# First cross attention: two heads in two row halves of TensorE, scores in two accumulated steps

## The reference

```python
def _L0_xattn_ref(q, k, v, Wq, bq, Wk, bk, Wv, bv, Wo, bo):   # q = layernorm(x), k = v = ctx_512 (4 x 4096 x 128)
    HEADS, D_K = 16, 16
    ...
    scores = jnp.einsum('bhqd,bhkd->bhqk', qh, kh) * scale
    attn = jax.nn.softmax(scores, axis=-1)
    out = jnp.einsum('bhqk,bhkd->bhqd', attn, vh)
```

## Time and profile before

| what | us |
|---|---|
| median of 3 runs | 1431.14 (1427.41 to 1432.78) |
| span of the profiled execution | 1429.1 |
| busy PE | 1375.6 |
| busy DVE | 1055.1 |
| busy ACT | 922.1 |
| busy POOL | 287.6 |

### The profile page before, as it was taken

How to read it: one execution, slowest core, us unless ns; L and a number is a source line. 1 busy time by engine, 2 the same in 40 slices (tenths; PEclk the granted TensorE clock), 3 DMA queues, 4 the chain that set the end, 5 groups by cost and what they waited for, 6 DMA issues and landing times.

```text
span 1429.1 us, 28070 instructions
## 1 busy us (share of the span) xinstructions
PE 1375.6 (96%) x11138; PEld 846.7 (59%) x11138; DVE 1055.1 (74%) x2114; ACT 922.1 (65%) x1899; POOL 287.6 (20%) x321
## 2 busy tenths in 40 slices
PE   7799999999999999999999999999999999989998
PEld 5355555555555545555554556556557999856666
DVE  4787777787777778777778888835876778767757
ACT  5366777767777767777767666672796664448731
POOL 3354222222222222122213100000003100001210
PEclk9899999999999999999999999999999999999999
DMA  6966555346554545655454743002402320347000
GB/s 184 163 145 143 119 118 111 77 102 130 116 127 92 102 84 125 128 115 113 81 97 101 184 73 61 2 1 60 119 18 65 112 67 1 91 112 155 2 1 30
DMA packets 95587, 133.19 MB, mean 93 GB/s; under 512 B 8864, under 2 KB 70944, under 8 KB 89504
## 3 DMA queue, kind: packets, MB, share of 16 engines
q1 hardware_dynamic: 95456, 131.40, 42.3%
HBM read 94.15 MB, written 37.22 MB: 92 GB/s over the span
## 4 chain that ended last, share of the span: by engine, by line
PE 79%; ACT 8%; DVE 8%; DMA 2%; issue 2%; SPq 1%; POOL 0%; DVEq 0%; ACTq 0%
PE psum L559 16%; PE psum L540 13%; PE psum L524 13%; ACT probs L783 4%; PE psum L2132 4%; PE psum L587 3%; PE psum L2106 3%; DVE peaks L685 3%; PE psum L626 3%; PE psum L1226 2%; PE psum L2851 2%; PE psum L1623 1%; PE psum L275 1%; PE psum L2861 1%; PE psum L2814 1%
## 5 line engine op out<-in xcount | busy, mean ns | idle before, releaser
L685 DVE TENSOR_REDUCE peaks<-psum 128x1 f32<-128x512 f32 x1024 | 643.3, 684 | 197.0 <-PE psum L524 196.4
L783 ACT ACTIVATE probs<-psum 128x512 f32<-128x512 f32 x1024 | 529.0, 615 | 83.3 <-PE psum L540 79.4
L524 PE MATMUL psum<-keysT,queriesT 96*128 96x512 bf16 x1024 | 390.1, 384 | 13.2 <-DMA keysT<-key_parts 7.9
L540 PE MATMUL psum<-queriesT,keysT 98*128 98x256 bf16 x2048 | 392.4, 274 | 6.1 <-ACT queriesT L846 2.4
L540 PEld LDWEIGHTS psum<-queriesT,keysT 98*128 98x128 bf16 x2048 | 176.3, 99 | 191.7 <-ACT probs L783 72.1
L559 PE MATMUL psum<-probs,values 128*17 128x256 f32 x4096 | 245.9, 380 | 0.0
L559 PEld LDWEIGHTS psum<-probs,values 128*17 128x17 f32 x4096 | 107.2, 97 | 102.6 <-issue 27.1
L524 PEld LDWEIGHTS psum<-keysT,queriesT 96*128 96x128 bf16 x1024 | 98.6, 96 | 90.9 <-issue 56.1
L918 POOL CAST key_parts<-key_f 128x512 bf16<-128x512 f32 x57 | 34.8, 611 | 518.0 <-ACT key_f L816 511.0
L816 ACT ACTIVATE key_f<-psum,bk 128x512 f32<-128x512 f32 x59 | 40.5, 687 | 120.7 <-PE psum L587 120.6
L587 PE MATMUL psum<-ctxT,wk 128*128 128x512 f32 x128 | 69.5, 625 | 2.4 <-DVE probs L728 0.9
(11 more groups left out here) (315 smaller groups left out, 1662.5 us busy)
## 6 DMA issues: line engine op xcount, KB each, us to landing
keysT<-key_parts SPq DMA_DIRECT2D x31, 768.0 KB, 7.7
key_parts<-key_parts SPq DMA_DIRECT2D x90, 256.0 KB
keysT<-key_parts SPq DMA_DIRECT2D x31, 512.0 KB, 10.1
ctx_nat<-in_ctx_dram SPq DMA_DIRECT2D x32, 256.0 KB, 3.0
keysT<-key_parts SPq DMA_DIRECT2D x31, 256.0 KB, 11.6
ctx_in<-in_ctx_dram SPq DMA_DIRECT2D x24, 256.0 KB, 5.9
ctx_turned<-ctxT SPq DMA_DIRECT2D x24, 256.0 KB, 4.4
ctx_T<-ctx_turned SPq DMA_DIRECT2D x12, 512.0 KB, 3.8
```

Of the source, the lines that this page charges most:

```text
L524: e.matmul(ps, self.queriesT[0:ROWS, u % 2, g * GH + j, t * P:(t + 1) * P], self.keysT[0:ROWS, i % RING, j, c * BANK:(c + 1) * BANK], star ...
L540: made = e.matmul(ps[:, j * S:(j + 1) * S], self.keysT[0:AUG, i % RING, j, kt * P:(kt + 1) * P], self.queriesT[0:AUG, u % 2, g * GH + j, : ...
L685: e.tensor_reduce(self.peaks[:, i % 2, pair, c:c + 1], k.ps(("max", n)), AX.X, ALU.max).then_inc(*self.peaked.up(n))
L783: e.activation(self.probs[:, t % RINGP, e2 * GH * S:(e2 + 1) * GH * S], k.ps(("scores", t, e2)), ACT.Exp).then_inc(*self.exped.up((t, e2)))
```

## The change

Each head gets its own row half of 64 rows. `keysT` and `queriesT` now have two planes: in MAIN four part products of a head (64 rows), in REST the other two part products and the two rows of ones and shift (34 rows). Head 0 lies at row 0, head 1 at row 64. A maximum is found from the MAIN plane alone, so from four part products; the maxima of the two heads follow each other. Scores are made for each head in its own bank (both 128-key tiles of the slot side by side), each in two accumulated steps, MAIN and REST, with the heads alternating; the banks still rotate over three, `SCORES[(2 * t + j) % 3]`. All eight score products of a slot stand ahead of the maxima, and the values burst behind both maxima. An exponential now covers one head of the slot, and each head has semaphores of its own for maxima and for scores. The copy of the turned shift becomes two. The parts are stored in an order in which the high and middle parts of the keys are one run of 32 rows, read twice for MAIN; the parts of the queries are stored five times instead of three.

```diff
-PAIRS = 6
-ROWS = PAIRS * DH
-AUG = ROWS + 2
+KEY_AT = (1, 2, 0)
+QUERY_AT = ((2, 3), (0, 1), (4,))
+HALF = P // 2
+MAIN, REST = 0, 1
+LOW = 2 * DH
+TALL = LOW + 2
...
-HALVES, SUMS = 3, 3
+SCORES, SUMS, BLOCK = (0, 1, 2), 3, 4
...
-        self.keysT = sb(scope, "keysT", [P, RING, GH, LC], BF16)
+        self.keysT = sb(scope, "keysT", [P, 2, RING, LC], BF16)
-        self.queriesT = sb(scope, "queriesT", [P, 2, P // DH, S], BF16)
+        self.queriesT = sb(scope, "queriesT", [P, 2, 2, UNIT_GROUPS, S], BF16)
...
-            i, r = divmod(n, MAXES)
-            pair, c = self.max_at(n)
-            j, t = divmod(pair, QT)
+            i, j, qt, c = self.max_at(n)
             u, g = divmod(i, UNIT_GROUPS)
+            own = slice(j * HALF, (j + 1) * HALF)
             job, let_go = ("max", n), (self.peaked, n)
             ps = banks.use(4 + n % 3, w, job, let_go) if now < -1 else misc(now, job, let_go)
             w.wait_ge(self.rows_here[u % 2], u)
             else:
                 w.wait_ge(self.pieces_here[c * self.PIECES // CH], 0)
-            e.matmul(ps, self.queriesT[0:ROWS, u % 2, g * GH + j, t * P:(t + 1) * P],
-                     self.keysT[0:ROWS, i % RING, j, c * BANK:(c + 1) * BANK],
-                     start=True, stop=True).then_inc(*self.max_made.up(n))
+            e.matmul(ps, self.queriesT[own, MAIN, u % 2, g, qt * P:(qt + 1) * P],
+                     self.keysT[own, MAIN, i % RING, c * BANK:(c + 1) * BANK],
+                     start=True, stop=True).then_inc(*self.max_made[j].up(n))
 
         for t in range(FIRST, TOTAL + 3):
             maxima = self.maxima(t)
...
                 u, g = divmod(i, UNIT_GROUPS)
                 w.wait_ge(self.shiftT_kept, i)
                 w.wait_ge(self.ones_in, 0)
-            for e2 in range(2):
-                if 0 <= t < TOTAL:
-                    kt, n = 2 * p + e2, (2 * t + e2) % HALVES
-                    ps = banks.use(n, w, ("scores", t, e2), (self.exped, (t, e2)))
-                    for j in range(GH):
-                        made = e.matmul(ps[:, j * S:(j + 1) * S], self.keysT[0:AUG, i % RING, j, kt * P:(kt + 1) * P],
-                                        self.queriesT[0:AUG, u % 2, g * GH + j, :], start=True, stop=True)
-                    made.then_inc(*self.scored.up((t, e2)))
-                if maxima and not e2:
-                    find_max(maxima[0], t)
-            if t % 4 == 1 and 5 <= t <= TOTAL + 1:
-                i, p0 = divmod(t - 5, SLOTS)
+                ps = {}
+                for e2 in range(2):
+                    kt = 2 * p + e2
+                    for plane, rows in ((MAIN, HALF), (REST, TALL)):
+                        for j in range(GH):
+                            if j not in ps:
+                                ps[j] = banks.use(SCORES[(2 * t + j) % len(SCORES)], w, ("scores", t, j), (self.exped, (t, j)))
+                            own = slice(j * HALF, j * HALF + rows)
+                            made = e.matmul(ps[j][:, e2 * S:(e2 + 1) * S], self.keysT[own, plane, i % RING, kt * P:(kt + 1) * P],
+                                            self.queriesT[own, plane, u % 2, g, :], start=(plane == MAIN), stop=(plane == REST))
+                            if e2 and plane == REST:
+                                made.then_inc(*self.scored[j].up((t, j)))
+            for n in maxima:
+                find_max(n, t)
+            if t % BLOCK == 1 and BLOCK + 1 <= t <= TOTAL + 1:
+                i, p0 = divmod(t - BLOCK - 1, SLOTS)
                 b, g = divmod(i, NG)
                 w.wait_ge(self.exped, (t - 2, 1))
-                for p in range(p0, p0 + 4):
+                for p in range(p0, p0 + BLOCK):
                     w.wait_ge(self.v_kept, (b, p))
                 w.wait_ge(self.ones_set, b % 2)
                 if i:
                     w.wait_ge(self.outT_kept, i - 1)
                 w.wait_ge(self.cleared, 0)
-                for p in range(p0, p0 + 4):
+                for p in range(p0, p0 + BLOCK):
                     for e2 in range(2):
                         for j in range(GH):
-                            quad, kt = e2 * GH + j, 2 * p + e2
+                            quad, half, kt = e2 * GH + j, 2 * j + e2, 2 * p + e2
                             made = e.matmul(k.bank(SUMS)[32 * quad:32 * quad + DH + 1, 0:S],
                                             self.values[b % 2][:, kt, g * GH + j, :],
-                                            self.probs[:, (SLOTS * i + p) % RINGP, quad * S:(quad + 1) * S],
+                                            self.probs[:, (SLOTS * i + p) % RINGP, half * S:(half + 1) * S],
                                             start=(p == 0), stop=(p == SLOTS - 1))
-                made.then_inc(*self.weighed.up((t - 5) // 4))
-            for n in maxima[1:]:
-                find_max(n, t)
+                made.then_inc(*self.weighed.up((t - BLOCK - 1) // BLOCK))
             for job, *a in self.due.get(t, ()):
                 if job == "turn ctx":
...
                     for pair in range(GH * QT):
-                        made = e.transpose(ps[ROWS:AUG, pair * P:(pair + 1) * P], self.shift_b[:, i % 2, pair, :],
+                        j, qt = divmod(pair, QT)
+                        made = e.transpose(ps[j * HALF + LOW:j * HALF + TALL, qt * P:(qt + 1) * P], self.shift_b[:, i % 2, pair, :],
                                            self.ident_b[:, :])
                     made.then_inc(*self.shiftT_made.up(i))
                 elif job == "normalize":
...
-        return divmod(r, CH) if i else divmod(r, GH * QT)[::-1]
+        step, j = divmod(r, GH)
+        qt, c = divmod(step, CH) if i else divmod(step, QT)[::-1]
+        return i, j, qt, c
...
-                for e2 in range(2):
-                    w.wait_ge(self.scored, (t, e2))
-                    e.activation(self.probs[:, t % RINGP, e2 * GH * S:(e2 + 1) * GH * S], k.ps(("scores", t, e2)),
-                                 ACT.Exp).then_inc(*self.exped.up((t, e2)))
+                for j in range(GH):
+                    w.wait_ge(self.scored[j], (t, j))
+                    e.activation(self.probs[:, t % RINGP, 2 * j * S:(2 * j + 2) * S], k.ps(("scores", t, j)),
+                                 ACT.Exp).then_inc(*self.exped.up((t, j)))
...
-                    e.activation(self.queriesT[ROWS:AUG, u % 2, g * GH:(g + 1) * GH, :].rearrange("p h n -> p (h n)"),
-                                 k.ps(("shiftT", i)).bitcast(BF16)[ROWS:AUG, 0:GH * S], ACT.Copy).then_inc(
-                        *self.shiftT_kept.up(i))
+                    for j in range(GH):
+                        own = slice(j * HALF + LOW, j * HALF + TALL)
+                        e.activation(self.queriesT[own, REST, u % 2, g, :], k.ps(("shiftT", i)).bitcast(BF16)[own, 0:S],
+                                     ACT.Copy).then_inc(*self.shiftT_kept.up(i if j else ("first", i)))
...
-                        w.wait_ge(self.scored, (SLOTS * (i - RING + 1) - 1, 1))
+                        for j in range(GH):
+                            w.wait_ge(self.scored[j], (SLOTS * (i - RING + 1) - 1, j))
-                        e.dma_start(self.q_dram[b, :, n, :, :, :].rearrange("h d m n -> h d (m n)"),
-                                    self.q_parts[:, n, :]).then_inc(*self.q_out.up(b))
+                        for copy in QUERY_AT[n]:
+                            e.dma_start(self.q_dram[b, :, copy, :, :, :].rearrange("h d m n -> h d (m n)"),
+                                        self.q_parts[:, n, :]).then_inc(*self.q_out.up(b))
-                        w.wait_ge(self.scored, (UNIT * (u - 1) - 1, 1))
-                    for block, run in RUNS:
-                        e.dma_start(self.queriesT[block * DH:(block + run) * DH, u % 2, :, :],
-                                    self.q_dram[b, :, 0:run, :, m, :].rearrange("h i d n -> (i d) h n")).then_inc(
-                            *self.rows_here[u % 2].up(u))
+                        for j in range(GH):
+                            w.wait_ge(self.scored[j], (UNIT * (u - 1) - 1, j))
+                    for plane, rows, parts in ((MAIN, HALF, slice(0, 4)), (REST, LOW, slice(3, 5))):
+                        for j in range(GH):
+                            e.dma_start(self.queriesT[j * HALF:j * HALF + rows, plane, u % 2, :, :],
+                                        self.q_dram[b, j::GH, parts, :, m, :].rearrange("h i d n -> (i d) h n")).then_inc(
+                                *self.rows_here[u % 2].up(u))
...
-        for block, run in RUNS:
-            e.dma_start(self.keysT[block * DH:(block + run) * DH, i % RING, :, keys],
-                        self.key_dram[u, g * GH:(g + 1) * GH, PARTS - run:PARTS, :, keys].rearrange(
-                            "j i d n -> (i d) j n")).then_inc(*landed.up(key))
+        source = self.key_dram[u, g * GH:(g + 1) * GH, :, :, keys].rearrange("j i d n -> j (i d) n")
+        n = keys.stop - keys.start
```

(40 more changed lines are left out.)

1 line of the change is left out of this document (removed).

## The result

| | us |
|---|---|
| before, median of 4 runs | 1431.62 (1427.41 to 1432.78) |
| after, median of 4 runs | 1790.03 (1788.69 to 1792.23) |
| ratio | 1.251 (95% interval 1.249 to 1.254) |
| span of the profiled execution after | 1790.6 |

The account below looks back on a forecast made before the run. PE was taken as the bound; a shorter lead over ScalarE (+0.81 us per block) less 0.35 from side jobs gives +0.46, over 128 blocks +59: 1429.1 + 59 + 2 = 1490 us, range 1438 to 1545.

Parts of the forecast that it names:

- The rest: Key, query and ones transfers, weights and later stages: taken as 0 in all, -4 to +3 us for the lead-in.
- my four rivals: PE's work alone counts (0.15), it comes out even (0.08), halves run one after the other (0.04), the clock falls (0.02).
- The lead over ScalarE: Score banks: PE and ACT take turns, 1.18 us per slot; a block without side jobs 6.31 us against 5.50, +0.81.
- Side jobs: Key fills, values jobs, turned context, gathers, shifts and copies: 1.06 us per block against 1.41, so 0.35 back.
- Overlap of the row halves: Scores and maxima on PE: products and loads of different halves overlap fully; eight score products take 0.44 us per slot.
- My sign of being wrong: Block without side jobs under 5.5 us, L783 waits staying 40.8 us in 442, or eight score products over 0.6.
- The clock rival: The clock falls because PE stands 0.5 us at a time; it would cost hundreds of us; chance 0.02.
- The first rival: Bank wait does not bite in the score stage, PE's work alone counts: -86 us, 1345 us; chance 0.15.

Follow-up runs that it names:

- the plain-read run: Changed kernel, each head's MAIN plane of keys read by two plain transfers of 32 rows instead of one with an outermost repeat of 2: 1514.8 us, 1.060 of before.
- the edit that filled it here: Weighted values of one slot made in every slot, not four slots' in every fourth: 1417.7 us on the kernel with plain reads, 1474.0 on the kernel before.

## Why the prediction was wrong

- **The step that failed** is in "The rest": "Keys: 4 transfers for 3, the same 96 rows per head and 1.5 MB per group, issued 11 slots ahead". Bytes, rows and lead were right; I set the cost at 0 and never asked how long the transfer of another form takes. Before, a key transfer landed in 7.7 to 11.6 us by the page, and 11 slots are some 19 us. The new ones, 1.0 MB of a group on what the trace shows as two of the 16 DMA engines (a share of 0.13), bring the keys 29 us after their issue. That cost 275 us. Not one of my four rivals was about DMA, though the diff rewrites these lines; the 0.55 of DMA share in the earlier trace rows said that there was room in bandwidth, and nothing about a single transfer's time. The rule on leading repeats in the Trainium skill (DMA: Bandwidth & Descriptors, Rules for kernel authors), which I did not weigh, speaks against just this line of the diff.
- **The lead over ScalarE**, the mechanism that I built the forecast on, was right where it stands alone: 1.20 measured for 1.18, and 6.30 for 6.31, to the hundredth by some luck, since the slot behind the burst was taken 0.04 too long (1.31 for 1.35) and the two turns 0.02 too short each. The run with two banks in the kernel before and that with four in the changed one move it in both directions.
- **Side jobs** were mis-sized: 1847 score products in the stretch of the plain-read run are 57.7 blocks of 7.66 us, so 1.35 for side jobs and waits where I summed 1.06. Of the difference the clock is 0.15 at most (0.98 in that stretch: 0.04 of the 442 us at half speed are 18 us, half of them lost, over 57.7 blocks), and some is the shift's copy, which as two instructions holds ACT 0.78 us (343.50 to 344.28) ahead of a score's exponential. I did not take the rest apart. Over 128 blocks 0.29 would be 37 us; the kernel as a whole lost 83 against 59, 24 more.
- **Overlap of the row halves** was right: eight score products and the start of the maximum behind them lie 0.46 us apart (320.35 to 320.81), and seven behind a wait 0.34 (321.66 to 322.00). My sign of being wrong, eight score products over 0.6 us, must be read by starts: as busy time they show 0.62, with the drain of the last one in it.
- **The clock rival** came true (0.89 in the stretch) by another cause. I tied it to stalls of 0.5 us; with those alone, in the plain-read run, it is 0.98. It falls in the waits for keys (206.2 us in 33 waits, 6.2 in the mean): 0.50 from 558 to 561, in the wait of 5.87 us.
- **The first rival** (PE's work alone, 1345) is not reached by any run; the best is 1418, with the gap filled and every slot paying 0.23 to 0.27 us for its two changes of shape.

## What to carry to other kernels

A transfer whose source gets a new outermost dimension is a new transfer: read from the trace how long one of its kind takes to land before calling it hidden, even if bytes and rows are unchanged. When it is out, look at the DMA share of a short stretch in which it runs alone: an average over a longer one (0.25 to 0.37 here) hid the two engines that 0.13 shows. When two banks are opened at once and completed at once, count the turn from completion to completion against the consumer: three banks then gave a turn of 1.20 us here, two banks opened one after the other 1.08. A gap of fixed length in each step can be filled with work already there; the edit that filled it here (-97 us) costs 43 us where there is no gap.

## What the runs showed of the hardware

- A group's 1.5 MB of keys, 1.0 of them in the MAIN plane: with the repeat of 2 outermost there, the DMA share is 0.13 where these transfers run nearly alone (two engines of 16), and the keys came after 29 us; as plain transfers of 32 rows, 0.88 to 1.06 and 8 us.
- Cut in two along the keys, the same transfers still show a share of 0.14 and bring the keys 26 to 29 us after the first issue (29 to 34 uncut); SP's two issues behind them took 6.80 us instead of 0.89.
- A change from full-height products to the column quarters of the values and back cost 0.22 us in the kernel before with values in every slot, and one from the row halves and back 0.23 to 0.27 us.
- Row halves overlap with bf16 products of 64 and 34 rows too, which no row of before showed: eight of 256 columns and the start of the next product lie 0.46 us apart (320.35 to 320.81).
- The clock kept 0.98 in a stretch full of waits of 0.3 to 0.5 us; it stood at 0.89 and 0.86 in those with a wait for keys in each group, 6 us in the mean in the one and 10 in the other.
